# Shifted-window attention on one core: q and k one image ahead, key blocks on GpSimd, weighted values in tiles of 18 columns, another lead-in

## The reference

```
xn  = layernorm(x) * g + b                       # over the 96 channels
xw  = windows(roll(xn, (-4, -4)))                # 4 windows of 64 tokens per image
q, k, v = split(xw @ qkv_w + qkv_b);  q = q * SCALE
attn = softmax(q @ k.T + rel_bias + shift_mask)  # per window and head, 64 x 64
x   = x + unroll((attn @ v) @ proj_w + proj_b)
```

## Time and profile before

| | |
|---|---|
| median of 3 runs | 491.94 us (491.89 to 494.11) |
| profiled execution | 491.68 us |
| its span, first to last instruction | 490.0 us |
| busy share of the span | PE 97%, PEld 63%, DVE 75%, ACT 60%, POOL 38% |
| instructions | 21340 |

### The profile page before, as it was taken

How to read it: one execution, slowest core, us unless ns; L and a number is a source line. 1 busy time by engine, 2 the same in 40 slices (tenths; PEclk the granted TensorE clock), 3 DMA queues, 4 the chain that set the end, 5 groups by cost and what they waited for, 6 DMA issues and landing times. The chain is left out here.

```text
span 490.0 us, 21340 instructions
## 1 busy us (share of the span) xinstructions
PE 475.3 (97%) x8006; PEld 308.8 (63%) x8006; DVE 366.1 (75%) x1013; ACT 294.8 (60%) x757; POOL 186.0 (38%) x230
## 2 busy tenths in 40 slices
PE   8999999999999999999969999999899999999996
PEld 7777777777777777777844344344566666666663
DVE  1599999999999999999873546654966666666553
ACT  2477877787778778877656747642344344444332
POOL 8634343434344434443333012652232333433300
PEclk9999999999999999999999999999999999999998
DMA  4210111111101110110004543475445444444411
GB/s 79 72 36 18 34 33 46 21 33 33 30 19 32 32 27 21 32 32 1 4 7 98 93 105 89 117 181 131 108 111 131 120 107 132 120 111 125 121 41 33
DMA packets 41963, 33.29 MB, mean 68 GB/s; under 512 B 19456, under 2 KB 37760, under 8 KB 41920
## 3 DMA queue, kind: packets, MB, share of 16 engines
q1 hardware_dynamic: 37952, 26.21, 21.5%
q0 software_dynamic: 3968, 6.51, 5.8%
HBM read 19.25 MB, written 7.13 MB: 54 GB/s over the span
## 5 line engine op out<-in xcount | busy, mean ns | idle before, releaser
L379 POOL TENSOR_TENSOR scores<-scores,peak 128x768 f32<-128x768 f32 x64 | 94.2, 1472 | 129.6 <-DVE peak L548 129.6
L1542 PE MATMUL banks<-x_stack,conv_w 40*32 40x256 f32 (+1 forms) x2304 | 97.0, 380 | 0.0
L1017 POOL DMA_DIRECT2D x_stack<-padded_x x96 | 52.3, 548 | 94.6 <-PE banks L1542 56.4
L442 ACT COPY probs_t<-ps_probs 128x768 f32<-128x768 f32 x64 | 51.1, 798 | 40.3 <-PE ps_probs L704 40.2
L1542 PEld LDWEIGHTS banks<-x_stack,conv_w 40*32 40x32 f32 (+1 forms) x2304 | 51.7, 107 | 26.9 <-issue 11.3
L540 DVE TENSOR_TENSOR scores<-ps_scores,bias 128x768 f32<-128x768 f32 x64 | 61.3, 957 | 5.3 <-PE ps_scores L694 3.5
L548 DVE TENSOR_REDUCE peak<-scores 128x12 f32<-128x768 f32 x64 | 61.0, 953 | 2.4
L717 PE MATMUL ps_out<-v_blocks,probs_t 128*64 128x54 f32 x1536 | 57.2, 224 | 0.6 <-ACT out_t L447 0.6
L717 PEld LDWEIGHTS ps_out<-v_blocks,probs_t 128*64 128x64 f32 x1536 | 50.2, 138 | 11.8 <-issue 11.7
L436 ACT ACTIVATE scores<-scores 128x768 f32<-128x768 f32 x64 | 54.2, 847 | 1.5 <-POOL scores L379 1.5
L704 PE MATMUL ps_probs<-ident,scores 128*128 128x128 f32 x384 | 54.3, 277 | 0.0
(11 more groups left out here) (146 smaller groups left out, 809.8 us busy)
## 6 DMA issues: line engine op xcount, KB each, us to landing
x_stack<-padded_x SPq DMA_DIRECT2D x96, 54.0 KB
x_stack<-padded_x POOLq DMA_DIRECT2D x96, 54.0 KB, 2.7
padded_x<-x_pad SPq DMA_DIRECT2D x32, 121.5 KB, 2.5
stream<-y_sliced SPq DMA_DIRECT2D x48, 64.0 KB, 2.8
out<-y_sb SPq DMA_DIRECT2D x32, 96.0 KB, 1.9
x_now<-in_x SPq DMA_DIRECT2D x32, 72.0 KB, 1.8
stream<-in_x SPq DMA_DIRECT2D x32, 72.0 KB, 1.9
x_sliced<-stream SPq DMA_DIRECT2D x36, 64.0 KB, 2.0
```

The source lines that it names most:

```text
L379: nc.gpsimd.tensor_tensor(sc, sc, peak[:, par, p, :].unsqueeze(2).to_broadcast((128, HEADS, WN)), ALU.subtract).then_inc(s["shifted"], 1)
L442: nc.scalar.copy(probs_t[:, :], ps_turned).then_inc(s["turned_copied"], 1)
L1017: engine.dma_start(x_stack[64 * half + i * HC:64 * half + (i + 1) * HC, slot, :, :], rows).then_inc(landed[slot], 16)
L1542: mm = nc.tensor.matmul(home, conv_w[rows, kind, j, k, :], grid(x_stack[rows, slot, k, :], PADW)[:, :, j:j + W], start=(j == 0), stop=(j = ...
```

## The change

- `make_q_and_k`, ACT's `copy_q` and DVE's part of k work on image t+3 instead of t+2 in step t; `turn_back` on t+4, `turn_tokens` and `measure` on t+5. `normed`, `q_sb` and `k_blocks` get two buffers. One more lead-in step (t = -5) stands in front, and one more image is unrolled at the end of the loop.
- DVE's `copy_k` becomes `move_k`, an add of the bias out of PSUM into `k_sb`, 96x256. POOL makes the masked blocks from it (`build_k`, 96x1024) a step ahead of their scores and ahead of that step's two subtractions. The blocks of images 0 and 1 are built by DVE as before (`build_first_k`).
- `score` waits for q's copy and k's move of the image after its own, since these read the banks that it writes, and for its own key blocks.
- `weigh` has four tiles of 32 columns of weights and 18 moving columns per pair of heads, 24 matmuls instead of 12. `v_blocks` loses its two spare pairs.
- In the lead-in, `score(0,0)` stands in step -3, `score(0,1)`, `make_v(0)` and `make_q_and_k(1)` in step -2, and three of the five groups of fills in the step loop (20 matmuls) go.

```diff
@@ led_image_loop
+    step(-5, -3, 1)
     step(-4, -2, 0)
...
-    image_loop(engine, step, tail=2)
+    image_loop(engine, step, tail=3)
@@ buffers
-    normed = sb("normed", [C, N])
-    q_sb = sb("q_sb", [C, N])
-    k_blocks = sb("k_blocks", [C, GROUP, N])
-    v_blocks = sb("v_blocks", [128, 2, PAIRS, 2, HP + 2, 2, VC])
+    normed = sb("normed", [C, 2, N])
+    q_sb = sb("q_sb", [C, 2, N])
+    k_sb = sb("k_sb", [C, N])
+    k_blocks = sb("k_blocks", [C, 2, GROUP, N])
+    v_blocks = sb("v_blocks", [128, 2, PAIRS, 2, HP, 2, VC])
@@ gpsimd
+        def build_k(t, par):
+            pool.wait_ge(s["k_moved"], t - 1)
+            need(pool, s["scores_ready"], (t - 1) * 2)
+            nc.gpsimd.tensor_tensor(k_blocks[:, par, :, :], k_sb[:, :].unsqueeze(1).to_broadcast((C, GROUP, N)),
+                                    head_mask[:, :].unsqueeze(2).to_broadcast((C, GROUP, N)), ALU.mult).then_inc(s["k_built"], 1)
+
         def step(t, half, par):
+            if real(t + 1) and not is_image(t, 0):
+                build_k(t + 1, 1 - par)
             subtract_peak(t, 0, par)
             subtract_peak(t, 1, par)
@@ vector
-        def copy_k(t):
+        def move_k(t):
             dve.wait_ge(s["k_ready"], t + 1)
-            need(dve, s["scores_ready"], t * 2)
-            nc.vector.scalar_tensor_tensor(out=k_blocks[:, :, :], in0=ps_k.unsqueeze(1).to_broadcast((C, GROUP, N)),
+            need(dve, s["k_built"], t - 2)
+            nc.vector.tensor_scalar(k_sb[:, :], ps_k, b_k[:, 0:1], None, ALU.add).then_inc(s["k_moved"], 1)
...
         def step(t, half, par):
-            if real(t + 3):
+            if real(t + 4):
                 gather_spread()
+            if is_image(t, -4):
+                prepare()
             if is_image(t, -3):
-                prepare()
-            if real(t + 2):
-                copy_k(t + 2)
+                build_first_k(0)
+            if real(t + 3) and not is_image(t, -2) and not is_image(t, -3):
+                move_k(t + 3)
...
+            if is_image(t, -2):
+                find_peak(0, 1, 0)
+                build_first_k(1)
+            if real(t + 5):
+                measure(t + 5)
+                await_stats(t + 5)
+            if real(t + 2) and not is_image(t, -2):
                 find_peak(t + 2, 1, par)
@@ tensor
-        def make_q_and_k(t):
+        def make_q_and_k(t, par):
...
+            if is_image(t, 1):
+                pe.wait_ge(s["biased"], 2)
+            if is_image(t, 2):
+                pe.wait_ge(s["q_copied"], 2)
+                pe.wait_ge(first_built, 2)
+            need(pe, s["biased"], (t - 1) * 2)
...
-        def score(t, p):
+        def score(t, p, par):
             u = t * 2 + p
-            pe.wait_ge(s["q_copied"], t + 1)
-            pe.wait_ge(s["k_copied"], t + 1)
+            if is_image(t, 0):
+                pe.wait_ge(s["q_copied"], 1)
+                pe.wait_ge(first_built, 1)
+            else:
+                pe.wait_ge(s["q_copied"], up_to(t + 1))
+                pe.wait_ge(s["k_moved"], up_to(t + 1) - 2)
+                if is_image(t, 1):
+                    pe.wait_ge(first_built, 2)
+                else:
+                    pe.wait_ge(s["k_built"], t - 1)
@@ weigh
             for q in range(HP):
-                for top in range(2):
-                    mm = nc.tensor.matmul(ps_out[64 * top:64 * top + 64, 0, q * 2 * VC:(q + 3) * 2 * VC],
-                                          probs_t[:, q * 128 + 64 * top:q * 128 + 64 * top + 64],
-                                          v_blocks[:, par, p, top, q:q + 3, :, :].rearrange("p q e c -> p (q e c)"),
+                for part in range(4):
+                    at = q * 128 + 32 * part
+                    mm = nc.tensor.matmul(ps_out[32 * part:32 * part + 32, 0, q * 2 * VC:(q + 1) * 2 * VC],
+                                          probs_t[:, at:at + 32],
+                                          v_blocks[:, par, p, part // 2, q, :, :].rearrange("p e c -> p (e c)"),
                                           start=True, stop=True, skip_group_check=True)
@@ step of tensor
-            if real(t + 2):
-                make_q_and_k(t + 2)
+            if real(t + 3) and not is_image(t, -2):
+                make_q_and_k(t + 3, 1 - par)
...
             if is_image(t, -2):
-                fill(nc, free, blank[:, :], 10)
-            if real(t + 2):
-                score(t + 2, 0)
-            if is_image(t, -2):
+                score(0, 1, 0)
                 fold_v()
+                make_v(0, 0)
+                make_q_and_k(1, 1)
+            if real(t + 2) and not is_image(t, -2):
+                score(t + 2, 0, par)
```

More of the change, by code:

```diff
@@ L277, in window_attention @@
     zeroed = sem("zeroed")
+    first_built = sem("first_built")
     blanked = sem("blanked")
@@ L419, in copy_q @@
             act.wait_ge(s["q_ready"], t + 1)
-            need(act, s["scores_ready"], t * 2)
-            nc.scalar.activation(q_sb[:, :], ps_q, ACT.Identity, bias=b_q[:, 0:1], scale=SCALE).then_inc(s["q_copied"], 1)
+            need(act, s["scores_ready"], (t - 1) * 2)
+            nc.scalar.activation(q_sb[:, par, :], ps_q, ACT.Identity, bias=b_q[:, 0:1], scale=SCALE).then_inc(s["q_copied"], 1)
         def copy_v(t, par):
@@ L430, in copy_v @@
                 half = slice(64 * e, 64 * e + 64)
-                nc.scalar.copy(v_blocks[half, par, :, :, 0:HP, e, 0:HD].rearrange("p a b q d -> p (a b) q d"),
+                nc.scalar.copy(v_blocks[half, par, :, :, :, e, 0:HD].rearrange("p a b q d -> p (a b) q d"),
                                ps_v[half]).then_inc(s["v_copied"], 1)
@@ L802, in step @@
                 fold_fc1(2)
-            if is_image(t, -3):
+            if is_image(t, -4):
                 fill(nc, free, blank[:, :], 8)
-            if real(t + 3):
-                turn_back(t + 3)
-            if real(t + 2):
-                make_v(t + 2)
+            if real(t + 4):
+                turn_back(t + 4)
+            if real(t + 2) and not is_image(t, -2):
+                make_v(t + 2, par)
             if real(t + 1):
                 weigh(t + 1, 0, 1 - par)
-            if is_image(t, -2):
-                fill(nc, free, blank[:, :], 4)
-            if real(t + 2):
-                score(t + 2, 1)
-            if real(t + 4):
-                turn_tokens(t + 4, half + 2, par)
-            if is_image(t, -3):
+            if is_image(t, -3):
+                score(0, 0, 0)
+            if real(t + 2) and not is_image(t, -2):
+                score(t + 2, 1, par)
+            if real(t + 5):
+                turn_tokens(t + 5, half + 2 + par, 1 - par)
+            if is_image(t, -4):
                 fold_q_k_v()
                 fold_mean()
-                fill(nc, free, blank[:, :], 6)
-            if is_image(t, -2):
                 fill(nc, free, blank[:, :], 6)
```

45 lines of the change are left out of this document (23 added, 22 removed).

## The result

The changed kernel takes **486.5 us** in the median of 4 runs (485.3 to 487.6), the kernel before 493.0 beside it on the same chip (491.9 to 499.0). The ratio of their undisturbed runs is on record as 0.989, 95% interval 0.985 to 0.993. The profiled execution took 486.64 us, its span 484.7. So it is faster, as forecast, but by 1% and some 6 us where I had written 17, and the range (467.5 to 484.0) missed it.

The account below looks back on a forecast made before the run. It took a loop through q, score and two bias adds, with PE and DVE nearly full, as the bound. Images -20.1, last images -0.5, lead-in +3.5 gave -17.1 us against 491.68, so 474.8 us in the median; range 467.5 to 484.

Parts of the forecast that it names:

- The loop: Steady image: q, score, two bias adds and back to q bind after the change, at 6.34 us an image.
- 0.16 us is lost per image: Score in the steady image: PE waits for DVE's key blocks; the change removes this 0.16 us.
- 48 x 8.75 = 0.42 us: New weigh: 48 records at the channel stage gram's 8.75 ns each, so each weigh becomes 0.42 us shorter.
- A cost at nothing: PE's order in a step: unchanged, and pieces apart from weigh keep their matmuls, so no added cost.
- Key blocks and POOL: Block building: DVE's add takes 0.42 us busy, POOL's product 1.90 us, and it just fits ahead of subtract(0).
- q and k one image ahead: Step order with two buffers: loads are asked for one step earlier; costed at nothing.
- Lead-in: Before the steady images: new order costs 1.5 us and a later clock rise 2 (0 to 5), together +3.5.
- Tail: Last two images: two shorter weighs each, partly hidden, -0.5 us.
- Weigh doesn't shrink: Rival: columns of weights set weigh's cost, so PE binds at 6.84 us an image; 490.5 us, chance 0.08.
- In between: Weigh shrinks only to 0.6 us, loop 6.52 us, 480 us in all; chance 0.05.
- POOL and issue: Rivals: POOL's product takes 2.7 to 2.9 us, 479.5, chance 0.06; records cost 31 ns each, about 530, chance 0.04.
- The clock as a rival: Thinner matmuls leave PE at the lower level, stage gains over 100 us; only the lead-in looks exposed; chance 0.05.

Follow-up runs that it names:

- tokens twice: Changed kernel with twenty lead-in fills put back, the two transpositions of turn_tokens issued twice; 487.4 us, ratio 0.988.
- windows half of `make_v`: Changed kernel with twenty lead-in fills put back, make_v run only for windows 0 and 1 from image 1 on; 479.1 us, a single run.
- first kernel with fills: Changed kernel with twenty fill matmuls put back in PE's idle places of the lead-in, first measurement; 481.5 us, ratio 0.974.

## Why the prediction was right in sign and wrong in size

My 474.8 stood on a span 17.1 us shorter; it became 5.3 shorter. Of the 11.8 us between, 7.8 lie in the images, 3.2 in the lead-in and 0.8 in the tail.

- **The loop.** That q, score, the two bias adds and back to q would bind was right, with every leg behind the score: 0.85, 2.31 (forecast 2.37), 0.96, 0.14. The leg from q to score(0) took 2.34 instead of 2.02, and 2.34 + 0.85 + 2.31 + 0.96 + 0.14 = 6.60. Of the 0.32 us too little, 0.14 are `turn`, 0.13 weigh, both below, and 0.05 q: from q's start to k's are 0.47 us where q starts right behind the bias add, and 0.43 in the runs where the bias add isn't what holds it (before, old weigh, tokens twice). The windows half of `make_v` confirms the loop.
- **"0.16 us is lost per image" to the wait for the key blocks.** This step failed. I had compared `turn` followed by project (0.65) with `turn` followed by score (0.81) and taken the blocks' end, 0.16 us ahead of the score, as its cause. With everything ready 0.6 us early, the 0.77 to 0.81 is still there. Most of the difference comes with what follows. From `turn`'s last start to the next start are 0.20 us ahead of score and 0.11 ahead of project, in the kernel before, in the changed one and in that with the old weigh alike (0.45 where score really waits); project uses 96 rows and columns, score 32-row tiles. The rest, 0.04 to 0.05 us, lies within `turn`: behind a weigh its records take longer to start than behind `turn_tokens`. The blocks' nearness was a coincidence, and 7.0 us was PE's own sum. That the shape of the next tiles is the cause rests on where the extra time appears, here and in the next two points, and from `turn_back` to `make_v` (0.20 too); no run changed the shape of score's tiles. The Trainium skill (TensorEngine Tiling (Array Packing), Key Properties) says that a change of the tiling mode, unlike a change of tile, drains TensorE. It gives no time; the handovers measured here agree with it: beyond the spacing that the group's own records have, 0.07 to 0.13 us with a change of tile shape and nothing without (`make_v` to the old weigh, gram to the group behind it, `turn` to project). I had not weighed that rule.
- **"48 x 8.75 = 0.42 us" for weigh.** The spacing was right (9.0 ns), the term was mis-sized: I set the gram's first-to-next time against weigh's and left out the handover to another tiling, 0.13 to 0.14 us, which gram's neighbour doesn't need. The first weigh of a step saved 0.29 us and not 0.42. The second saved 0.24, since it had held PE for 0.80 before and not for 0.84, as I had taken both.
- **A cost at nothing.** `make_v` to weigh became 0.60 from 0.50. The old weigh had `make_v`'s 64-column tiles and started 0.05 us after its last record's start (130.60 to 130.65); the new one starts 0.15 us after it (131.44 to 131.59). This 0.10 us lies off the leg from q to score and thus cost PE's sum, not the loop: 7.01 - 0.29 - 0.24 + 0.10 = 6.58, and 6.57 was measured. Forecast was 6.00.
- **Key blocks and POOL.** Right: 1.89 us for 1.90, 0.45 for 0.42 on DVE, and no wait of score for the blocks. The gain of this half is the step from 6.85, DVE's sum with the blocks, to 6.61. DVE's own image without them wasn't reached by any run.
- **q and k one image ahead** bring nothing to the image on their own: with the blocks on DVE and the short weigh it is 6.85 with or without it. No run has POOL's product, which is made a step ahead of its scores, without it.
- **Lead-in.** The order cost 1.7 to 2.0 us (forecast 1.5); score(1,0), which I had at 25.6 us, starts at 25.85 in the first kernel with fills. The clock cost 5.2 to 6.2 (forecast 2, bound 5). I had taken the rise to be late by a few microseconds of PE's work. In the profiled execution it didn't come until 34.3 us. Waits on DVE kept PE idle in part of that time (1.80 us ahead of score(0,1), 0.29 ahead of q(1)), but it stayed away for another 9 us in which PE was never idle. With the fills in those places it came at 13 to 15 us; what holds it back without them stays open.
- **Tail.** The last images gave 1.0 us (the MLP's first group starts 15.3 us after weigh(30,1), 16.3 before), the clock took 1.7 back there; what follows that group is 0.3 shorter.
- **The rivals.** Weigh doesn't shrink: its price (490.5) wasn't reached, nor its 0.84. "In between" (weigh 0.6, loop 6.52, 480 us) came nearest in mechanism, and I gave it 0.05; with 6.60 for its 6.52 (2.4 us) and 3.2 more for the lead-in it gives 485.6, about where the kernel landed. POOL and issue are out: 1.89 us, 9.0 ns. The clock as a rival is out for the images (1.00 from 100 to 150 us), but its last sentence, that the lead-in looks exposed, was right. The Trainium skill (TensorE: Matmul & The Clock Gate, "Wait — 56ns, not 53.3ns?") has 25 ns between starts as its floor; the trace disagrees for matmuls on four different column tiles.

With the period right and my lead-in (30 x 0.41 = 12.3 against 20.1) the sum would have been 482.6, and the version with the fills back, whose lead-in is as I had thought, takes 481.2 to 481.5.

## What to carry to other kernels

A group's time from its start to the next group's start holds the handover to that next group. Before carrying a rate per record to another place, ask whether the neighbour there has the same tiles, and cost the handover apart. A piece that ends just ahead of a start is not yet what it waited for: look for an idle time in the record, or for the same pair of pieces elsewhere with the supposed releaser long done. Where two bounds lie within 3% of each other (here PE's 7.0 and DVE's 6.85, afterwards the loop's 6.61 and PE's 6.57), work out both for each half of a change, since either half alone may give nothing. And matmuls nobody reads may carry the clock: taking twenty out cost 0.4 us before and 5 to 6 us with the new order, and neither could be told ahead from how long the engine stands idle. Measure the lead-in by itself, and count it from a piece behind which the edit begins, since executions differ by a microsecond ahead of it.

## What the runs showed of the hardware

- Records of 32-column matmuls, dealt in turn to four column tiles, start on average 8.5 ns (gram) and 8.9 ns (weigh) apart with 12 moving columns and 9.0 with 18; 64-column ones in two tiles with 54 and 48 moving columns start 28 to 30 ns apart. Eight 64-column records all on one tile take as long as sixteen over two (0.59 and 0.60 us to the next group).
- From the last start of weigh, `make_v` or gram, a group on the same tiles follows after 0.01 or 0.05 us, and one on other tiles or the whole array after 0.13 to 0.15. From the last transposition of `turn` or `turn_back`, a group on tiles follows after 0.20 us, and a 96x96 matmul after 0.11.
- The granted clock stayed at half level from about 10 to 34 us with PE 82% busy in the middle of it (12.28 of 15 us) and busy without a gap in its last 9 us, and in the same place stood at full level with fills in the gaps (0.97 to 1.00 from 15 us on). In the same program run again it was at full level from 13.6 to 17 us in between.
- The same lower level showed at the MLP's entry behind 2.85 us of idle PE in the changed kernel and was absent behind 3.21 in the kernel before. It was absent as well behind 2.84 us in the changed kernel with the old weigh (8.25 us for the group) and present behind 3.22 in the kernel before with the short one (9.94). What decides there isn't settled; ten fills in the gap brought the full level in the one execution that was profiled.
